# Splitting the row-shifted copy of a convolution block between ScalarE and GpSimd

## The reference, cut to what matters

```
x_f    = fft2(gn(x))                                   # depthwise, circular
gate_A = sigmoid(ifft(gA_f * x_f))                     # 7 x 7 kernels, one per channel
gate_B = sigmoid(ifft(gB_f * x_f))
b_t    = ifft(B_f * x_f) * gate_B
h      = (8 steps of a gated scan of softplus(b_t))
x      = x + h @ W_out + b_out
```

## Time and profile before

| | us |
|---|---|
| median of 3 runs | 6728.38 (6723.05 to 6730.23) |
| the profiled execution, its time | 6717.27 |
| its span | 6715.5 |
| TensorE busy | 5725.9 (85%) |
| GpSimd busy | 4125.6 (61%) |
| VectorE busy | 4511.4 (67%) |
| ScalarE busy | 3640.0 (54%) |

### The profile page before, as it was taken

The page is one execution under the profiler, slowest core; times in us unless marked ns, Lnnn a source line. Parts: engine busy times, 40 slices in busy tenths (PEclk is TensorE's granted clock), DMA queues, the critical chain, the costliest instruction groups (busy, mean ns, idle before and its releaser), DMA issues. The chain is left out here.

```text
span 6715.5 us, 144257 instructions
## 1 busy us (share of the span) xinstructions
PE 5725.9 (85%) x51796; PEld 5234.1 (78%) x51796; DVE 4511.4 (67%) x5284; ACT 3640.0 (54%) x4872; POOL 4125.6 (61%) x3608
## 2 busy tenths in 40 slices
PE   5789999999999999999984368888888888888887
PEld 5678888888888888888874368777877878777787
DVE  6367777777777777777763786666666666666653
ACT  5555555555555555555540445555555555555554
POOL 0146666666666666666667677676676767676751
PEclk8899999999999999999997789999999999999999
DMA  5356676666766667666656469899999999999987
GB/s 130 123 157 205 205 216 202 206 198 207 212 209 199 200 206 211 207 198 207 190 168 184 122 176 262 252 261 249 259 261 253 265 255 262 245 256 251 258 247 212
DMA packets 1239334, 1441.35 MB, mean 215 GB/s; under 512 B 142960, under 2 KB 1025396, under 8 KB 1238516
## 3 DMA queue, kind: packets, MB, share of 16 engines
q1 hardware_dynamic: 1238516, 1431.07, 75.0%
HBM read 999.09 MB, written 431.64 MB: 213 GB/s over the span
## 5 line engine op out<-in xcount | busy, mean ns | idle before, releaser
L1257 PE MATMUL psC<-wide,xhl 128*128 128x256 bf16 x6144 | 1037.1, 279 | 37.1 <-DVE xhl L1455 15.2
L1187 POOL TENSOR_TENSOR stage<-stage,nrow 128x1024 f32<-128x1024 f32 x240 | 620.0, 2583 | 407.8 <-DMA stage<-x_by_block_row 397.0
L1254 PE MATMUL psC<-wide,xhl 128*128 128x192 bf16 x6144 | 863.3, 250 | 0.0
L1204 POOL COPY down<-xhl 48x448 f32<-48x448 f32 x512 | 533.2, 1041 | 520.9 <-PE psC L1263 421.9
L813 POOL TENSOR_TENSOR y<-y,grow 128x1024 f32<-128x1024 f32 x256 | 603.9, 2359 | 323.7 <-DVE y L657 323.7
L1455 DVE SCALAR_TENSOR_TENSOR xhl<-xhl,psC 128x512 f32<-128x512 f32 x512 | 348.8, 682 | 503.7 <-ACT xhl L1348 503.0
L824 POOL TENSOR_TENSOR q<-q,qinv 128x1024 f32<-128x1024 f32 x256 | 490.0, 1914 | 308.6 <-DVE qinv L731 308.6
L1263 PE MATMUL psC<-narrow,down 128*128 128x96 bf16 x6144 | 527.3, 210 | 171.5 <-DMA narrow<-toeplitz_narrow 98.1
L657 DVE TENSOR_TENSOR y<-psProj,rstd 128x1024 f32<-128x1024 f32 x256 | 313.5, 1225 | 516.0 <-POOL rstd L805 516.0
L1348 ACT ACTIVATE xhl<-psC 128x512 f32<-128x512 f32 x512 | 304.3, 599 | 636.7 <-PE psC L1263 635.1
L1254 PEld LDWEIGHTS psC<-wide,xhl 128*128 128x128 bf16 x6144 | 639.3, 115 | 12.2
(11 more groups left out here) (181 smaller groups left out, 14276.2 us busy)
## 6 DMA issues: line engine op xcount, KB each, us to landing
wide<-toeplitz_wide SPq DMA_DIRECT2D x1024, 140.0 KB, 4.5
xa<-in_x SPq DMA_DIRECT2D x256, 512.0 KB, 4.7
xb<-in_x SPq DMA_DIRECT2D x256, 512.0 KB, 3.8
xc<-in_x SPq DMA_DIRECT2D x256, 512.0 KB, 5.7
x_rows<-xc SPq DMA_DIRECT2D x256, 512.0 KB
res<-x_rows SPq DMA_DIRECT2D x256, 512.0 KB, 7.2
out<-res SPq DMA_DIRECT2D x256, 512.0 KB, 6.4
stage<-x_by_block_row SPq DMA_DIRECT2D x225, 512.0 KB, 7.2
```

Of the source, the lines that this page charges most:

```text
L1187: nc.gpsimd.tensor_tensor(v, v, nrow[:, 0:1, :].to_broadcast([P, NP_, C]), ALU.mult).then_inc(s_scaled, 1)
L1204: nc.gpsimd.tensor_copy(dst[lo, :, :, 0:last], src[lo, :, 0:NQ, CW:])
L1254: nc.tensor.matmul(dst[:, :, :, 2:], lhs, tab[:, :, 32 + part * 12:44 + part * 12], start=False, stop=False)
L1257: nc.tensor.matmul(dst, lhs, tab[:, :, part * 16:part * 16 + 16], start=(n == 0), stop=False)
```

## The change

The two copies of partitions 0 to 47 leave GpSimd. ScalarE makes them, in bf16 and not in f32 words, in a new function `own_rows`, behind the tanh of every odd slot, and behind its set-up before image 0 for the first two blocks. TensorE waits for a further semaphore.

```
@@ gpsimd, move_down @@
-                nc.gpsimd.tensor_copy(dst[lo, :, :, 0:last], src[lo, :, 0:NQ, CW:])
-                nc.gpsimd.tensor_copy(dst[lo, :, :, last:], src[lo, :, 0:NQ, 0:CW])
                 nc.gpsimd.tensor_copy(dst[hi, :, :, 0:last], src[lo, :, 1:NQ + 1, CW:])
                 nc.gpsimd.tensor_copy(dst[hi, :, :, last:], src[lo, :, 1:NQ + 1, 0:CW]).then_inc(s_down, 1)
@@ tensor, conv_second @@
                 pe.wait_ge(s_down, img * NBLK + blk + 1)
+                pe.wait_ge(s_own, img * NBLK + blk + 1)
@@ scalar @@
+            def own_rows(img, par, blk):
+                act.wait_ge(s_chain, 3)
+                count = img * NBLK + blk - DR + 1
+                if known(count):
+                    act.wait_ge(conv_ready, count)
+                if blk == 0:
+                    act.wait_ge(s_wrap, img + 1)
+                    act.wait_ge(xl_done, img * NST + NST)
+                if not isinstance(img, int):
+                    act.sem_inc(s_own_go, 1)
+                src = xhl[par][:, blk].rearrange("p a (q m) e -> p a q (m e)", q=NQ + 1)
+                dst = down[:, blk % DR].rearrange("p a (q m) e -> p a q (m e)", q=NQ)
+                lo, last = slice(0, NARROW_J), (NP_ - 1) * CB
+                nc.scalar.copy(dst[lo, :, :, 0:last], src[lo, :, 0:NQ, CB:])
+                nc.scalar.copy(dst[lo, :, :, last:], src[lo, :, 0:NQ, 0:CB]).then_inc(s_own, 1)
@@ scalar, image @@
                             gate(img, par, blk)
+                            if blk + DR < NBLK:
+                                own_rows(img, par, blk + DR)
+                            elif has_stage:
+                                own_rows(img + 1, 1 - par, blk + DR - NBLK)
                         if blk % BPG == 0 and g and has_conv:
                             expo(img, g - 1)
@@ scalar, before image 0 @@
             for i in range(NST - 4, IMGS):
                 window(i)
+            for blk in range(DR):
+                own_rows(0, 0, blk)
```

More of the change, by code:

```diff
@@ L956, in layer1 @@
         s_go = sem("d_down_begun")
+        s_own = sem("d_down_own_column")
+        s_own_go = sem("d_down_own_begun")
         s_res = [sem(f"d_res{k}") for k in range(RES)]
```

## The result

The changed kernel is slower: 6815.1 us median against 6729.3, 86 us more, a ratio of 1.0124 (95% interval 1.0107 to 1.0142). Forecast were 40 us more: 6768, in a range of 6675 to 6880. The direction and the place were right; the loss was more than twice the forecast one.

What follows compares the result with a forecast made beforehand. Bound: TensorE's work plus 63.1 us of idle time in two images. Fifteen images at 4.3 - 0.8 us give +52, the first image -12, total +40 on 6728: 6768 us, range 6675 to 6880.

Steps and rivals of the forecast that it cites:

- Price of the copies: On ScalarE, two added bf16 copies per block: 0.93 and 0.27 us, holding the engine 1.0 us, bounds 0.7 to 1.6.
- Place: ScalarE's switch from tanh through Exp and Ln to the next tanh: 9 us where it took 7.92.
- GpSimd's relief: Two copies fewer per block on GpSimd: 0.8 us gained per image in the loop, 12 us in the first image.
- the sum 15 x (4.3 - 0.8) - 12: Whole kernel: fifteen images of delay kept less GpSimd's gain, +52 us, less 12 in the first image; total +40 us.
- 8.0 x 0.54 = 4.3 us stay: Per image, eight ScalarE switches each 1.0 us later; 46% of TensorE's idle time is late transfers, which absorb part.
- but there is slack: Copies behind the tanh after the second table load delay cast and evacuation by 2.0 us; ScalarE idled 1.08 us there.
- Image 0: First image: TensorE waited 58.4 us for GpSimd's copies; 12 us of gain taken, bounds 0 and 58.
- 13.8 us of idle time: First image: VectorE, with only this much idle in the 165 us shown, becomes the limit once GpSimd has fewer copies.
- GpSimd's wait for stages would shrink: Loop sign: GpSimd's wait for stages, 54.8 us in two images before, shrinks; no size given.
- Faster: Loop: transfers would have held TensorE anyway, so ScalarE's delay vanishes and GpSimd's relief stays; 6644 to 6704 us, chance 0.29.
- no change: Whole kernel: relief and delay cancel, absorption near 85%; 6728 us within 13 us, chance 0.13.
- Backlog: ScalarE's switch: two blocks' pairs, 2.0 us, both land there, delaying a needed evacuation, nothing absorbed; +216, 6944 us, chance 0.09.

Runs made afterwards that it cites:

- m_after_exp: Changed kernel with the own-column copies of every fourth block, those ScalarE made between tanh and Exp, back on GpSimd; 6729.6 us, ratio 1.0003.
- m_switch_only: Changed kernel with ScalarE making only every fourth block's own-column copies, between tanh and Exp, GpSimd the rest; 6792.4 us, ratio 1.0095.
- relief: Kernel before with GpSimd's two copies dropped and made by nobody, so part of the convolution is left out; 6721.9 us, ratio 0.9988.
- load: Changed kernel with GpSimd still making four copies per block, two of them spare; 6818.4 us, ratio 1.0132.
- fill: Changed kernel with TensorE running products whose result is overwritten ahead of five long-awaited transposes per image; 6792.2 us, ratio 1.0097.
- m_late: Changed kernel with the pair before the Exp moved behind the Ln and the next slot's hT evacuation; 6838.4 us, ratio 1.0158.

## Why the prediction was too small

- **Price of the copies: right.** Forecast 0.93 and 0.27 us, 1.0 us for both; measured 0.93 and 0.30, and the Exp 1.02 us later. The changed kernel's ScalarE is busy 267.9 us in two images, forecast "about 270". GpSimd has 166.8, forecast between 150 and 195.
- **Place: right.** The switch takes 8.93 us (forecast 9), and VectorE waits 81.0 us for the tanh (forecast "towards 80"). m_after_exp and m_switch_only show that the pair before the Exp is the cause.
- **GpSimd's relief: small, as forecast, but far smaller than the sum had it.** Forecast were 12 us over the loop and 12 in image 0, 24 together; `relief` gives 5 by its medians and at most 17 by its interval, with image 0 in it. Its 13 images took 2334.0 us in the profiled execution, against 2329.3 before. The first copy left did inherit the waiting: the third copy's mean rose from 683 ns to 1010 (L1206, 64 of them, changed kernel), near the 1057 of the former first. That agrees with the port pair that the Trainium skill ("SBUF — State Buffer", Who interferes with whom) calls an exclusive lock of VectorE and GpSimd, though no view here names the VectorE instruction that held a copy up.
- **The step that failed: the sum 15 x (4.3 - 0.8) - 12, in two of its terms.** The delay was put at 15 x 4.3 = 64 us, from "8.0 x 0.54 = 4.3 us stay"; `load`, which has the delay and no relief, shows 92 (77 to 100). Most of what is missing is the second pair, whose place behind the tanh was put at nothing: "but there is slack". It costs 12 to 23 us in the experiments above. The slack of 1.08 us in the earlier trace rows was real, but it was one example. The other term is the relief of 24 us, of which about 5 came. 28 us too little delay and 19 too much relief make up the 46 us by which the forecast fell short, within the measurement.
- **The 4.3 us: right in size for the pair before the Exp, by luck.** `m_switch_only` costs 65 us, or 4.3 per image. But I had worked the 4.3 out as idle time of TensorE, less what transfers give back, and the loss came as slower work. In the 13 images of `m_switch_only` TensorE's idle time rose by 7.6 us and its busy time by 48.2; in the changed kernel idle time rose by 4.8 us and busy time by 68.9. The giving back did take place in the changed kernel: TensorE's waits for the narrow table fell from 80.8 to 69.4 us, those for the wide table from 12.1 to 6.0, VectorE's for the scaling from 308.8 to 187.8 (210.6 in `load`, so mostly not by GpSimd's relief). But stalls of 2 to 5.5 us replaced shorter ones, and TensorE's clock fell to half behind them. Nor is the clock alone the cause: `fill` restored it and got back about a quarter of the loss, because TensorE's waits behind the late switch stay (before transposes about 146 us with the products in them, 57.6 before the change). Idle and clock are one budget here; the limit is ScalarE's switch, and TensorE may spend its waiting time standing or working slowly.
- **Image 0: 12 us forecast, 2.3 measured.** The 58.4 us of waits for GpSimd's copies vanished, and others took their place at once (before, the narrow table held TensorE 6.3 us there and the product not at all):

```profile
PE psC L1263 <- DMA narrow<-toeplitz_narrow: 42.1, 17, 5.5
PE psC L1257 <- DVE xhl L1478: 17.2, 9, 3.7
```

The narrow loads stand in SP's queue behind stage loads, and SP waits there for VectorE's low halves: 68.5 us in 3775 to 3945 us, and 65.4 already before the change. `relief` shows the same two waits (44.3 and 17.9 us) and an image 0 of 180.1 us, so they come with GpSimd's copies gone and not with ScalarE's. That VectorE is the limit, as I wrote, fits this but was not tested by itself; its 13.8 us of idle time were not to be had.
- **An indicator that was wrong:** I wrote that GpSimd's wait for stages would shrink. It grew from 54.8 to 84.9 us, because GpSimd itself arrives earlier: over the 13 images it is 367.8 us before, 629.4 in `relief` and 326.0 in `load`.
- **The rivals.** Faster and no change fell. Backlog named what the forecast had left out, the second pair in a switch, but at 8 us per image, where 12 to 23 us in all, about 1 per image, were measured.

What stays open: how the 73.7 us would divide between clock and waits without the added products, since `fill` puts work of its own on TensorE; and which single instruction of the late switch and of the chain behind it carries the loss, since `m_late` did not separate the evacuations from the tanh.

## What to carry to other kernels

Before an instruction is moved to an engine with idle time, look for the stretch in which that engine's queue is late, and keep the instruction out of it: the pairs of all four blocks cost 86 us, and 2 us, within the measurement, when the one pair in front of the Exp stayed on GpSimd. Slack read from one example is not a budget: the pair behind the second tanh, put at nothing, cost 12 to 23 us. And when waits are traded, look at their length as well as their sum, because TensorE's granted clock fell behind many of the long ones here.

## What the runs showed of the hardware

TensorE's granted clock fell from 2.4 to 1.2 GHz behind stalls as short as 2.0 to 2.7 us in the changed kernel; in its two images this happened behind all five stalls of that length that ended on f32 transposes, as at 5023.11 us. In the kernel before it stayed at 2.4 GHz behind a stall of 2.35 us that ended on such transposes, at 4875.43. The time at 1.2 GHz in the 13 images rose from 109 to 273 us while the idle time rose by 4.8 us. Products with throwaway results in those waits brought the mean clock from 0.94 to 0.98. ScalarE's copies of 48 partitions cost what 128 partitions with as many elements would by its other rows, and never varied much: 920 to 951 ns over 512 copies, while GpSimd's varied from 552 to 2607.
